# The two half-row matmuls of an upsampling block made one step of the plan, in two neighbouring banks

## What is computed

```
x = x + L0(groupnorm(x))    # upsample 2x in h and w (Fourier), 96 -> 384 -> h*h polynomial -> 96, low-pass, take every second pixel
x = x + L1(groupnorm(x))    # Mamba over the 4096 tokens: in-projection, 3-tap convolution, SiLU, dt/B/C, scan with 16 states, gate, out-projection
h = dA_t * h + dBu_t        # the scan: 192 channels x 16 states, one after the other over 4096 tokens
```

## Time and profile before

| | |
|---|---|
| three runs | 6277.81, 6282.98, 6292.53 us; median 6282.98 us |
| the profiled execution | 6281.37 us, its span 6279.6 us |
| busy share of the span | PE 96%, DVE 90%, POOL 83%, ACT 81% |
| mean granted clock of TensorE | 0.964 of full |
| instructions in the span | 99521 |

### The profile page before, as it was taken

One profiled execution on the slowest core, in us unless ns is written; L12 is line 12 of the kernel. 1 busy time (PEld: TensorE's weight loads), 2 busy tenths in 40 slices (PEclk: granted clock), 3 DMA queues, 4 the chain that ended last, 5 costly groups with the idle time before them and its releaser, 6 DMA issues. The chain is left out here.

```text
span 6279.6 us, 99521 instructions
## 1 busy us (share of the span) xinstructions
PE 6000.8 (96%) x32251; PEld 3116.7 (50%) x32251; DVE 5683.0 (90%) x4450; ACT 5094.3 (81%) x8658; POOL 5215.4 (83%) x5092
## 2 busy tenths in 40 slices
PE   8999999999999999999999999999999999998776
PEld 5645545454554545555455555545455454544222
DVE  0089999999999999999999999999999999999998
ACT  4588888888888888888888888888888888887664
POOL 0078888888888888888888888888888888888887
PEclk9999999999999999999999999999999999998665
DMA  3367676676767667676776767667676766766553
GB/s 95 89 167 174 161 172 155 168 166 165 172 156 169 158 168 169 160 180 145 173 162 161 175 156 180 150 167 166 163 171 163 171 158 164 167 147 157 131 118 75
DMA packets 805829, 983.27 MB, mean 157 GB/s; under 512 B 391259, under 2 KB 417543, under 8 KB 805319
## 3 DMA queue, kind: packets, MB, share of 16 engines
q1 hardware_dynamic: 805318, 976.92, 66.3%
HBM read 717.71 MB, written 259.00 MB: 156 GB/s over the span
## 5 line engine op out<-in xcount | busy, mean ns | idle before, releaser
L1183 POOL TENSOR_TENSOR hc<-hs,cs 128x512 f32<-128x512 f32 x3072 | 3840.8, 1273 | 631.0 <-DVE hs L1142 486.7
L1142 DVE TENSOR_TENSOR_SCAN hs<-av,state,b 128x512 f32<-128x512 f32 x2688 | 3257.6, 1263 | 84.0 <-DVE b L1136 1.8
L1008 ACT ACTIVATE av<-rep_d,nega 128x512 f32<-128x512 f32 x3072 | 2095.8, 713 | 33.2 <-DVE hs L1142 28.4
L1136 DVE TENSOR_TENSOR b<-rep_u,b 128x1536 f32<-128x1536 f32 x1024 | 1803.2, 1761 | 173.3 <-PE b L846 81.1
L855 PE MATMUL py<-hc,rsel 128*32 128x512 f32 x6144 | 1149.4, 638 | 12.5 <-POOL hc L1183 12.1
L769 PE MATMUL cb<-xu,w1a 96*128 96x392 f32 x2400 | 973.6, 509 | 0.9 <-ACT dlt L998 0.9
L774 PEld LDWEIGHTS cb<-w2c,g 128*98 128x98 f32 x9600 | 885.4, 167 | 147.1 <-issue 108.2
L774 PE MATMUL cb<-w2c,g 128*98 128x96 f32 x9600 | 908.0, 251 | 1.7 <-ACT g L956 1.7
L956 ACT ACTIVATE g<-cb,b1a 128x392 f32<-128x392 f32 x1200 | 680.3, 580 | 85.1 <-PE cb L769 76.7
L810 PE MATMUL cb<-xn,wtap 96*96 96x512 f32 x1536 | 721.9, 606 | 1.3 <-ACT xn L1029 1.0
L769 PEld LDWEIGHTS cb<-xu,w1a 96*128 96x128 f32 x2400 | 414.8, 190 | 373.8 <-issue 255.5
(11 more groups left out here) (109 smaller groups left out, 6674.1 us busy)
## 6 DMA issues: line engine op xcount, KB each, us to landing
rep_d<-delta_scratch SPq DMA_DIRECT2D x512, 384.0 KB, 7.3
rep_u<-deltax_scratch SPq DMA_DIRECT2D x512, 384.0 KB, 6.3
cs<-c_scratch SPq DMA_DIRECT2D x512, 256.0 KB, 5.9
delta_scratch<-dlt SPq DMA_DIRECT2D x128, 384.0 KB, 3.0
deltax_scratch<-dlt SPq DMA_DIRECT2D x128, 384.0 KB, 9.3
t1r<-t_scratch SPq DMA_DIRECT2D x160, 240.0 KB, 6.6
v_scratch<-v2s SPq DMA_DIRECT2D x192, 192.0 KB
xb<-in_x SPq DMA_DIRECT2D x128, 192.0 KB, 4.7
```

What stands on the lines that cost most here:

```text
L1008: act.activation(av[:, n % NAV, :], rep_d[:, k % 2, j, :], ACT.Exp, scale=nega[:, q, j:j + 1])\
L1136: dve.tensor_tensor(b3[:, 2::-1, :], of_hf[:, 2::-1, :], b3[:, 0:1, :].broadcast_to([128, 3, T]), ALU.mult).then_inc(dve_bu, 1)
L1142: dve.tensor_tensor_scan(hs[:, n % NHS, :], av[:, n % NAV, :], b3[:, n % 3, :], start, ALU.mult, ALU.add)\
L1183: pool.tensor_tensor(hc[:, n % NHC, :], hs[:, n % NHS, :], cs[:, k % 2, g % NQ, :], ALU.mult)\
```

## The change

`SA` and `SB` of a block get one position (`even` and `alone` now place groups of steps, and `single` makes a group of one step of all others). PE does both matmuls in the step `SA`, one behind the other, into banks i and i + 1, after a wait for both; each still counts up `pe_conv`. `SB` keeps its place in the ring and its bank, and issues nothing on PE. The assumed cost of each falls from 0.70 to 0.45 us, so `level` and `warm` also place the W steps and the idle matmuls of the S part anew. The numbers of matmuls, evictions and transfers stay, apart from the idle matmuls: 45 for 48 in a FULL pass.

```diff
--- before.py
+++ after.py
@@ -48,7 +48,7 @@
 def s_steps():
     out = []
     for b in range(HH // XB_H):
-        out += [("ST", b), ("SA", b), ("SB", b)]
+        out += [(("ST", b),), (("SA", b), ("SB", b))]
     return out
 
 
@@ -75,7 +75,7 @@
 X_AT, Z_AT, DBC_AT, DT_AT = (8, 10), (12, 11), 14, 18
 KEEP_FREE = tuple(range(9, 9))
 
-PE_US = {"ST": 0.45, "SA": 0.70, "SB": 0.70, "W_up": 0.70, "W_f": 0.71, "W_2": 2.10, "W_dn": 0.75, "D_lo": 1.20, "D_hi": 1.20,
+PE_US = {"ST": 0.45, "SA": 0.45, "SB": 0.45, "W_up": 0.70, "W_f": 0.71, "W_2": 2.10, "W_dn": 0.75, "D_lo": 1.20, "D_hi": 1.20,
          "X": 2.72, "Z": 0.92, "DBC": 1.82, "DT": 0.50, "OUT": 2.70, "WARM": 0.215}
 PE_PB, PE_RED = 0.22, 1.00
 
@@ -84,9 +84,13 @@
 OFFSET = {"S": 2, "D": 1}
 
 
-def even(steps, lo, hi):
+def even(groups, lo, hi):
     free = [p for p in range(lo, hi + 1) if p % NU not in KEEP_FREE]
-    return [(free[i * len(free) // len(steps)], st) for i, st in enumerate(steps)]
+    return [(free[i * len(free) // len(groups)], st) for i, steps in enumerate(groups) for st in steps]
+
+
+def single(steps):
+    return [(st,) for st in steps]
 
 
 def loads(lo, hi, rows):
@@ -144,12 +148,12 @@
     if s:
         rows += [(0, ("SLD", 0))] + even(s_steps(), 3, S_LAST) + [(S_LAST + 5, ("SG1", 0)), (S_LAST + 10, ("SG2", 0))]
     if d:
-        rows += [(DW_AT, ("DW", 0)), (D_FIRST - 6, ("DLD", 0)), (D_FIRST - 2, ("DG", 0))] + even(d_steps(), D_FIRST, D_LAST)
+        rows += [(DW_AT, ("DW", 0)), (D_FIRST - 6, ("DLD", 0)), (D_FIRST - 2, ("DG", 0))] + even(single(d_steps()), D_FIRST, D_LAST)
         rows += [(D_LAST + 5, ("DG1", 0)), (D_LAST + 10, ("DG2", 0))]
     if w_tail:
         rows += level(w[W_HEAD:], 0, W_LAST, rows + list(beside))
     if w_head:
-        rows += [(S_LAST + 4, ("WLD", 0)), (W_FIRST - 3, ("WG", 0))] + even(w[:2], W_FIRST - 8, W_FIRST - 6)
+        rows += [(S_LAST + 4, ("WLD", 0)), (W_FIRST - 3, ("WG", 0))] + even(single(w[:2]), W_FIRST - 8, W_FIRST - 6)
         rows += level(w[2:W_HEAD], W_FIRST, NC8 * NU - 1, rows + list(beside))
     return rows
 
@@ -190,8 +194,8 @@
 
 def alone(*streams):
     rows = []
-    for steps in streams:
-        rows += [(i / len(steps), st) for i, st in enumerate(steps)]
+    for groups in streams:
+        rows += [(i / len(groups), st) for i, steps in enumerate(groups) for st in steps]
     return padded(rows)
 
 
@@ -398,9 +402,9 @@
         HEAD = w_steps()[:W_HEAD] + [("WLD", 0), ("WG", 0)]
         SETUP_STEPS = RING
         N_SETUP = 12
-        BEFORE = [alone([("SLD", 0)] + s_steps() + [("SG1", 0), ("SG2", 0)]),
-                  alone([("WLD", 0), ("WG", 0)] + w_steps() + [("DW", 0)], [("SLD", 0)] + s_steps()),
-                  alone([("DLD", 0), ("DG", 0)] + d_steps() + [("DG1", 0), ("DG2", 0)], head_before()), plan_before()]
+        BEFORE = [alone(single([("SLD", 0)]) + s_steps() + single([("SG1", 0), ("SG2", 0)])),
+                  alone(single([("WLD", 0), ("WG", 0)] + w_steps() + [("DW", 0)]), single([("SLD", 0)]) + s_steps()),
+                  alone(single([("DLD", 0), ("DG", 0)] + d_steps() + [("DG1", 0), ("DG2", 0)]), single(head_before())), plan_before()]
         FIRST, FULL, TAIL, LAST = [plan_of(kind) for kind in ("first", "full", "tail", "last")]
         LOOPS = NS - 2
 
@@ -719,7 +723,8 @@
                 made = {"W_f": [("W_up", b)], "W_2": [("W_f", b, f) for f in range(NF)],
                         "W_dn": [("W_2", e) for e in range(2 * b, min(2 * b + 2, NB))],
                         "DBC": [("X", b, 0), ("X", b, 1)], "DT": [("DBC", b)]}.get(name, [])
-                for bank_free, n_free in st.freed_all([i - RING] + [st.find(m, key) for m in made]):
+                before = [i - RING] + [i + 1 - RING] * (name == "SA")
+                for bank_free, n_free in st.freed_all(before + [st.find(m, key) for m in made]):
                     pe.wait_ge(bank_free, n_free)
                 if name == "PAD":
                     pe.transpose(bank[0:C, 0:C], ident[0:C, 0:C], ident[0:C, 0:C]).then_inc(pe_conv, 1)
@@ -735,12 +740,15 @@
                     pe.wait_ge(xb_ld[b % 2], count(xb_ld[b % 2], x * 64 + (b // 2 + 1) * 16))
                     for j in range(4):
                         mm = pe.transpose(bank[0:C, 128 * j:128 * j + 128], xb[:, b % 2, j, :], ident[:, :])
-                elif name in ("SA", "SB"):
-
-                    r = int(name == "SB")
-                    half = slice(64 * r, 64 * r + 64)
-                    mm = pe.matmul(bank[0:GW, 0:4 * C], up_w[half, r, :],
-                                   xb[half, b % 2].rearrange("p i c -> p (i c)"), start=True, stop=True)
+                elif name == "SA":
+
+                    for r in range(2):
+                        half = slice(64 * r, 64 * r + 64)
+                        pe.matmul(cb[0:GW, (i + r) % RING, 0:4 * C], up_w[half, r, :],
+                                  xb[half, b % 2].rearrange("p i c -> p (i c)"), start=True, stop=True).then_inc(pe_conv, 1)
+                    return
+                elif name == "SB":
+                    return
                 elif name in ("SG1", "DG1"):
                     v = int(name == "DG1")
                     pe.wait_ge(dve_m[v], count(dve_m[v], x + 1))
```

## The result

The changed kernel takes 6226.99 us in the median of four runs (6224.4 to 6231.85), the kernel before 6282.07 us in the median of four (6277.81 to 6292.53). The ratio is 0.9911, 95% interval 0.9894 to 0.9928: 55 us or 0.9% faster. The forecast was 6237 us with a range of 6228 to 6262.

What follows compares the result with a forecast made beforehand. DVE was taken to bound the loop nearly everywhere, PE some microseconds per pass and the stretch ahead of the loop. From 6281.37 us, 7.1 ahead and 37.8 in the loop come off: 6236.5, said as 6237, range 6228 to 6262.

Steps and rivals of the forecast that it cites:

- take 2.7 x 14 = 37.8 us: Loop, S parts of 14 passes: 2.8 us of DVE's waits per pass can be won, 2.7 taken, 37.8 us in all.
- the single's cost of 0.90 us: PE, an S matmul standing alone: 0.81 us until the next operation plus 0.09 for its entry.
- DVE's floor for an S part: Loop, first 28 groups of a pass: DVE needs 156.6 + 4.7 + 0.4 = 161.7 us.
- all eight `bn_stats`: S part on DVE: eight groups with one `bn_stats`, each 0.59 us longer, 4.7 us of the floor.
- 0.82 us for the pair: PE, two adjacent S matmuls: they overlap and cost 0.82 us, 0.91 with entry, saving 0.89 per block.
- the 7.1 foretold: Stage W of sample 0, ahead of the loop: PE's saving of 8 x 0.89 = 7.1 us counts whole; ends 6 and 7.6.
- less 0.1 for waits that fall differently: S part of each pass: 0.1 us left for single waits that fall differently each time, so 2.7 of 2.8.
- the rest, which I had put at nothing: Pass after the S part: same plan, its waits for PE stay, 207.4 us as before.
- The clock in the S part: Rival, S part of the loop: TensorE's clock falls to half, at g18 for instance; 6245 to 6262 us, chance 0.12.
- Waits that move: Rival, loop: DVE waits at two or three new places instead; 6274 us, no change, chance 0.08.
- No overlap: Rival, loop: the second matmul has its own wait, so a pair costs 1.62 us; 6260 to 6278 us, chance 0.06.
- ACT holding the pair: Rival, blocks 0, 5, 7 beside `X`: late ACT evictions delay PE; 26 us slower, 6307 us, chance 0.04.

Runs made afterwards that it cites:

- serial: The changed kernel, but a pair's second matmul reads partitions 0 to 63 like the first, so the two can't overlap; 6249.7 us, ratio 0.9942 to the kernel before.
- second_wait: The changed kernel, but PE waits for the second bank only ahead of a pair's second matmul; 6225.4 us, ratio 0.9903 to the kernel before.

## Why the prediction was nearly right, and what it mis-sized

The mechanism held: a pair overlaps, ahead of the loop PE's saving counts whole, and in the loop it counts down to DVE's floor. What failed are sizes. The largest is the step "take 2.7 x 14 = 37.8 us", where 46.7 us were gained; the next is the single's cost of 0.90 us, which is 0.98.

**What bounds the kernel: right; the floor 0.4 us too high.** DVE's floor for an S part, put at 161.7 us, was reached and passed: the mean is 161.50, and from sample 1 on the profiled S parts lie between 161.26 and 162.06. I had priced all eight `bn_stats` at the 0.59 us of the earlier trace rows, where one stands between two scans. At g19 and g26 it stands behind the last scan, ahead of the products, and costs 0.4:

```profile
2272.50 1.76 DVE L1144 TENSOR_TENSOR b<-rep_u,b 128x1536 f32<-128x1536 f32 x1
2274.35 3.62 DVE L1150 TENSOR_TENSOR_SCAN hs<-av,state,b 128x512 f32<-128x512 f32 x3
2277.89 0.66 DVE L1114 BATCH_NORM_STATS2 bst<-x1s 96x6 f32<-96x512 f32 x1
2278.47 1.74 DVE L1144 TENSOR_TENSOR b<-rep_u,b 128x1536 f32<-128x1536 f32 x1
```

This group (g19) takes 5.97 us, not 6.17. The aggregate is there as I had added it: g26 with both takes 6.38.

**The pair's cost: right; a single's: too low.** I took 0.82 us for the pair and found 0.83. I took 0.90 us for a single, by its own time and its entry. Its exit costs 0.08 us too, so a single costs PE 0.98; the saving is 1.0 us per block (8.1 for eight), not 0.89. This is the step "So a single costs 0.81 + 0.09 = 0.90 us". Ahead of the loop the scan started 8.9 us earlier for the 7.1 foretold, above the end of 7.6 that I had set: 1.0 us of the difference is this step, and 0.8 us is when TensorE got fast in stage W, which was luck. In the loop it changes little, since PE has reserve there already; serial shows how much of that reserve there is: with 0.64 of the 1.0 us per block gone DVE pays 1.0 us per pass.

**The gain in the loop: right in kind, a fifth too small.** I took 2.7 us per pass: 2.8 down to the floor, less 0.1 for waits that fall differently. Found are 3.06 us in the S part of the 13 passes and 0.22 in the rest, which I had put at nothing. The 0.22 goes with the clock at g32: in passes of both kernels without a fall there the rest takes 207.03 to 207.07 us (but 207.38 and 207.42 in sample 1), with one 207.39 to 207.45, and it fell in 9 of the 13 passes before and in 2 after. The rest's plan is the same, and second_wait had 8 such passes with the changed plan, so this term is in part luck. The first pass gained 4.1 us, and I had priced it like the others, though its S part (167.9 us) lay further above the floor. Together 46.7 us in 14 passes for 37.8.

**The sum.** 8.9 + 46.7 = 55.6 us for 44.9. Of the 10.7 us between them 1.8 lie ahead of the loop and 8.9 in the loop: 13 x 0.36 = 4.7 in the S parts, the largest mis-sized term (the floor put too high, and the 0.1 us of reserve), 13 x 0.22 = 2.9 in the rest, 1.4 in the first pass. In the profiled execution the long TAIL hid 5.6 of them, which was luck the other way: only by it does that execution, 6231.85 us, lie in the range.

**The range: its low end was too near.** I had allowed 3 us per pass and 7.6 ahead of the loop, each its own end, 6281 - 42 - 7.6 = 6232, and set 6228. The first pass, the rest of the pass and the exit weren't in it, nor that executions of one kernel differ by 7 to 15 us, by TAIL's clock among others.

**The rivals.** The clock in the S part: not seen from sample 1 on in the changed kernel, where it doesn't fall at g17 and g18 without idle matmuls either; with the old costs it fell at g6 in 11 of 13 passes, for 0.2 us each in most. "In the S part it was 1.00" held for the sample of the earlier trace rows, but not for the first pass. Waits that move: of DVE for the spread there are two in the 13 S parts from sample 1 on, 0.9 and 0.2 us. No overlap: refuted by the rows of the pair; the kernel that has none (serial) is 22 us slower and still faster than before by 0.6%, so it was wrong to put it at 6260 to 6278; its pair took 1.46 us and not 1.62. ACT holding the pair: no such wait.

**The placing of the W steps.** I hadn't given it a share of its own. It is worth 0.3 us per pass with the pair, by the clock at g6, and costs 0.7 to 0.8 us per pass without it.

## What to carry to other kernels

Where two engines take turns as the bound, first read the floor of the other one from a stretch that lacks the work in question; what you take off an engine is worth the wait that it causes above that floor and no more, and the whole of it where nothing else runs. In these runs two matmuls on different halves of the partitions, with different banks, cost as much as one when they were neighbours, and an isolated one cost its entry and its exit besides, so price an operation by the starts of the one before and the one behind. A cost table that levels a plan has to be changed with the work that it prices: alone it made this kernel slower, and left out it let the clock fall in a place where it had stayed up.

## What the runs showed of the hardware that I had not expected

- A matmul on 64 partitions slows some neighbours: 0.31 us for 0.22 from a spread into it (medians of before's loop), and 0.75 us for 0.67 for the operation behind it. A spread into a reduce or a `W_dn`, which write 32 and 64 partitions, takes 0.31 to 0.32 us too; and from a reduce it is 0.52 us into S as into `W_f`, so there the entry costs nothing more.
- The second half of a pair costs 0.02 us even with a semaphore wait and an increment of its own, where one on the same half costs 0.64.
- The rest of TAIL, the same stretch of the same plan, took 208.3 to 214.4 us, with the moments at which TensorE's clock fell and rose: one full group behind a quiet one took 9.65 us at half of the clock and 5.61 at 0.96.
